# Dot-attention layers of a graph network: units in pairs for the weighted sum, and ScalarE's exponentials taken two units ahead

## The reference

```python
# layer 0, one head
Q, K, V = h @ W_q, h @ W_k, h @ W_v
scores = where(adj == 0, -1e9, Q @ K.T / 8)
x = x + softmax(scores) @ V
# layer 1, four heads
v, q, k = h @ Wv[i] + bv[i], h @ Wq[i] + bq[i], h @ Wk[i] + bk[i]
scores = leaky_relu(q @ k.T / 8, 0.2) + mask
x = x + leaky_relu(mean over heads of softmax(scores) @ v, 0.2)
# layer 2: additive attention; layer 3: a GAT layer with a residual and a layer norm
```

## Time and profile before

| what | value |
|---|---|
| median of 3 runs | 3531.48 us (3525.62 to 3535.83) |
| the profiled execution's own time | 3536.67 us |
| its span, first to last instruction | 3534.6 us |
| mean granted TensorE clock | 0.962 |
| TensorE matmul busy | 3064.6 us, 30972 instructions |
| VectorE busy | 3083.5 us |
| ScalarE busy | 2894.8 us |
| GpSimd busy | 1068.3 us |

### The profile page before, as it was taken

One profiled execution on the slowest core, in us unless ns is written; L12 is line 12 of the kernel. 1 busy time (PEld: TensorE's weight loads), 2 busy tenths in 40 slices (PEclk: granted clock), 3 DMA queues, 4 the chain that ended last, 5 costly groups with the idle time before them and its releaser, 6 DMA issues. The chain is left out here.

```text
span 3534.6 us, 78838 instructions
## 1 busy us (share of the span) xinstructions
PE 3064.6 (87%) x30972; PEld 1680.4 (48%) x30972; DVE 3083.5 (87%) x4791; ACT 2894.8 (82%) x3697; POOL 1068.3 (30%) x909
## 2 busy tenths in 40 slices
PE   7988999999999879898898898988988988987875
PEld 5765666666666633333333333333333333335664
DVE  7886887878888789999999999999999999985675
ACT  4546787778877769999999999998999999985665
POOL 4434666666666600000001000000001010006674
PEclk9998999999999989999999999999999999998797
DMA  7640000000000000000000000000000000002121
GB/s 246 222 139 16 20 21 22 21 18 24 21 21 19 14 10 10 10 10 10 10 10 10 10 10 10 10 10 10 10 10 10 8 9 10 13 4 68 58 60 33
DMA packets 68411, 111.58 MB, mean 32 GB/s; under 512 B 26452, under 2 KB 26582, under 8 KB 68054
## 3 DMA queue, kind: packets, MB, share of 16 engines
q1 hardware_dynamic: 68054, 106.69, 9.8%
HBM read 86.61 MB, written 18.87 MB: 30 GB/s over the span
## 5 line engine op out<-in xcount | busy, mean ns | idle before, releaser
L1107 ACT ACTIVATE l_scalar_ring<-l_w,l_r 128x1024 f32<-128x1024 f32 x1632 | 1713.1, 1142 | 37.5 <-DVE l_values L1153 27.7
L1221 DVE TENSOR_SCALAR l_vector_ring<-l_w_code,l_r_code 128x2048 f32<-128x2048 f32 x1232 | 1588.9, 1354 | 3.2 <-issue 0.2
L1044 PE MATMUL scores<-l_scalar_ring,l_signs 128*32 128x512 f32 x6528 | 793.5, 605 | 91.0 <-ACT l_scalar_ring L1107 90.7
L1054 PE MATMUL scores<-l_vector_ring,l_signs_code 128*32 128x512 f16 x9856 | 672.2, 394 | 138.3 <-DVE l_vector_ring L1221 137.6
L462 POOL TENSOR_TENSOR l_masked<-l_relu,mask 128x512 f32<-128x512 f32 x512 | 586.0, 1167 | 342.2 <-ACT l_relu L664 320.8
L250 ACT COPY probs_t<-turned 128x512 f32<-128x512 f32 x512 | 293.4, 586 | 467.1 <-PE turned L209 467.1
L1054 PEld LDWEIGHTS scores<-l_vector_ring,l_signs_code 128*32 128x32 bf16 x9856 | 242.7, 95 | 590.1 <-DVE l_vector_ring L1221 303.7
L277 ACT ACTIVATE l_probs<-l_logits,negmax 128x1024 f32<-128x1024 f32 x384 | 442.9, 1153 | 6.4 <-DVE negmax L268 6.4
L209 PE MATMUL turned<-ident,l_probs 128*128 128x128 f32 x3072 | 436.6, 287 | 12.1 <-issue 7.7
L1044 PEld LDWEIGHTS scores<-l_scalar_ring,l_signs 128*32 128x32 f32 x6528 | 200.0, 110 | 471.9 <-issue 264.8
L268 DVE CUSTOM_DVE_ANT_0 l_logits<-scores,l_masked,l_bound 128x1024 f32<-128x1024 f32 x256 | 328.1, 1282 | 63.2 <-POOL l_masked L462 42.8
(11 more groups left out here) (247 smaller groups left out, 3095.8 us busy)
## 6 DMA issues: line engine op xcount, KB each, us to landing
mask<-masks_kept SPq DMA_DIRECT2D x192, 256.0 KB, 2.6
l_adj<-adj SPq DMA_DIRECT2D x64, 512.0 KB, 5.9
masks_kept<-l_mask_ring SPq DMA_DIRECT2D x64, 256.0 KB, 4.8
x_res<-x SPq DMA_DIRECT2D x8, 256.0 KB, 5.1
out<-x_res SPq DMA_DIRECT2D x8, 256.0 KB, 2.9
l_h<-l_h SPq DMA_DIRECT2D x8, 128.0 KB, 2.9
l_kl<-l_dh SPq DMA_DIRECT2D x32, 2.0 KB, 1.8
l_kl<-l_dl SPq DMA_DIRECT2D x32, 2.0 KB, 1.8
```

Source lines behind the costliest of these rows:

```text
L1044: last = nc.tensor.matmul(s.scores[g * ROWS:(g + 1) * ROWS, buf, half, :], signs[:, window], scalar_ring[:, at % SCALAR_RING, g, halves[ha ...
L1054: last = nc.tensor.matmul(s.scores[g * ROWS:(g + 1) * ROWS, buf, half, :], signs_code[:, par, g % 2, window], parts(vector_ring[:, at % VE ...
L1107: last = nc.scalar.activation(scalar_ring[:, at % SCALAR_RING, g, :], w[:, par, :], ACT.Relu, bias=r[:, par, column:column + 1])
L1221: last = nc.vector.tensor_scalar(vector_ring[:, at % VECTOR_RING, g:g + 2, :], w_code[:, par, :, :], r_code[:, par, 0, column:column + 1], ...
```

## The change

It concerns the dot layers alone (`dot_layer` and `copy_half`), in four parts:

- **probs_t** of the dot layers is a buffer of their own with two slots, one for the even and one for the odd unit of a pair.
- **The weighted sum** is issued once in two units, at odd n. The even unit's sum stands in the lower 64 partitions of PSUM (column half 0), the odd one's in the upper; for each block of nodes the even unit's product is followed by the odd unit's. It waits for the half copies of both units.
- **One copy** of the sum (at odd n) and **one product** serve the pair. The product is issued after the turning of the next even n, and again at the graph's end. Its weights, `wv_pairs`, are 128 x 128 with the two heads' value weights on the diagonal (in layer 0 the same weights twice), so that 128 columns come out, 64 for each unit. VectorE finishes both units one after the other at even n, with a drain between them in layer 1.
- **The exponential** of ScalarE's iteration n is that of unit n+2; that of unit 1 is taken before the loop.

The order of VectorE's logits (n+2), ScalarE's relu (n+3), TensorE's scores (n+3), GpSimd's mask (n+3) and the fills is as before.

```diff
-def copy_half(eng, copy, s, sems, half, u):
+def copy_half(eng, copy, s, sems, half, u, to=None):
...
-    copy(s.probs_t[:, half * n:(half + 1) * n, :], s.turned[:, half * n:(half + 1) * n, :]
+    copy((s.probs_t if to is None else to)[:, half * n:(half + 1) * n, :], s.turned[:, half * n:(half + 1) * n, :]
...
+        wv_pairs = sb("wv_pairs", [P, PAIRED, P], F32)
+        probs_t = sb("probs_t", [P, 2, NB, P], F32)
...
-        unit_out = s.outT[:, P:P + D]
+        pair_out = s.outT[:, P:2 * P]
...
+            def turn_pair(q, p):
+
+                pe.wait_ge(sems["out_copied"], STARTS + q + 1)
+                wait(pe, sems["unit_done"], STARTS + 2 * q)
+                nc.tensor.matmul(pair_out, s.turned_out[:], wv_pairs[:, p % PAIRED, :], start=True, stop=True
+                                 ).then_inc(sems["out_turned"], 1)
+
+            def pair_times_values(par, q):
+
+                pe.wait_ge(sems["half0_copied"], STARTS + 2 * q + 2)
+                pe.wait_ge(sems["half1_copied"], STARTS + 2 * q + 2)
+                wait(pe, sems["out_copied"], STARTS + q)
+                wait(pe, sems["unit_done"], STARTS + 2 * q)
+                for j in range(NB):
+                    for odd in range(2):
+                        last = nc.tensor.matmul(s.outT[odd * D:(odd + 1) * D, 0:P], values[:, par, j, :], probs_t[:, odd, j, :],
+                                                start=(j == 0), stop=(j == NB - 1))
+                last.then_inc(sems["out_ready"], 1)
+
             def graph(b, par, project, last_graph):
                 for n in range(U):
                     u = b * U + n
                     turn_probs(pe, s, sems, probs[:, n % 2, :], u)
-                    if n > 0:
-                        turn_out(pe, s, sems, u - 1, 0, unit_out, weights=wv[:, (n - 1) % H, :])
+                    if n > 0 and n % 2 == 0:
+                        turn_pair(b * Q + n // 2 - 1, n // 2 - 1)
...
-                    wait(pe, sems["unit_done"], STARTS + u)
-                    if n == 0:
+                    if n == 1:
                         pe.wait_ge(sems["values_ready"], b + 1)
-                    probs_times_values(pe, s, sems, values[:, par, :, :], u)
-                turn_out(pe, s, sems, b * U + U - 1, 0, unit_out, weights=wv[:, H - 1, :])
+                    if n % 2:
+                        pair_times_values(par, b * Q + n // 2)
+                turn_pair(b * Q + Q - 1, Q - 1)
...
-                    copy_half(a, nc.scalar.copy, s, sems, 1, u)
-                    if not (last_graph and n + 1 == U):
-                        exponentials(a, s, sems, logits[:, (n + 1) % 2, :], probs[:, (n + 1) % 2, :],
-                                     (n + 1) % 4, u + 1)
+                    copy_half(a, nc.scalar.copy, s, sems, 1, u, probs_t[:, n % 2, :, :])
+                    if not (last_graph and n + 2 >= U):
+                        exponentials(a, s, sems, logits[:, n % 2, :], probs[:, n % 2, :], (n + 2) % 4, u + 2)
...
+            exponentials(a, s, sems, logits[:, 1, :], probs[:, 1, :], 1, 1)
...
-                    copy_half(v, nc.vector.tensor_copy, s, sems, 0, u)
-                    if n > 0:
+                    copy_half(v, nc.vector.tensor_copy, s, sems, 0, u, probs_t[:, n % 2, :, :])
+                    if n > 0 and n % 2 == 0:
+                        finish(b, n - 2, u - 2)
+                        if leaky:
+                            v.drain()
                         finish(b, n - 1, u - 1)
...
-                    copy_out(v, s, sems, u)
+                    if n % 2:
+                        copy_out(v, s, sems, b * Q + n // 2)
...
+                v.drain()
+                finish(b, U - 2, b * U + U - 2)
                 v.drain()
                 finish(b, U - 1, b * U + U - 1)
...
+            nc.vector.memset(wv_pairs[:], 0.0)
+            v.drain()
             v.wait_ge(sems["weights_in"], 16 * WEIGHT_LOADS)
+            for odd in range(2):
+                rows = slice(odd * D, (odd + 1) * D)
+                nc.vector.tensor_copy(wv_pairs[rows, :, rows], wv[rows, min(odd, H - 1):H:2, :])
```

More of the change, by code:

```diff
@@ L321, in dot_layer @@
     CONST = float(D)
+    PAIRED = max(1, H // 2)
+    Q = U // 2
     with ExitStack() as ctx:
@@ L759, in finish @@
                 slot = n % 4
-                v.wait_ge(sems["out_turned"], u + 1)
+                v.wait_ge(sems["out_turned"], b * Q + n // 2 + 1)
                 xb = s.block(b, i)
+                unit_out = pair_out[:, n % 2 * D:(n % 2 + 1) * D]
                 if not leaky:
```

## The result

The changed kernel takes 4171.69 us (median of 4 runs, 4158.55 to 4178.85), the kernel before 3533.65 beside it: a ratio of 1.179, with a 95% interval of 1.177 to 1.182. It is slower by 638 us. 4170 us was forecast, in a range of 4060 to 4290.

A forecast was written before the change was run, and what follows sets the result against it. The prediction took TensorE and VectorE in turn to bound layer 1 before, and a ring through three engines after. Terms 495 + 85 + 40 + 2 + 18 = 640 us gave 4170 us, 18% slower, range 4060 to 4290.

The forecast's parts named there:

- ring: Layer 1: logits u, exponential u, relu u+1, mask u+1, logits u+1, once per unit; 5.60 us a step, +495 us.
- steps after fills: Layer 1: evictions of the next graph's projection also wait behind logits; 6.17 us, or 7.04 before a fourth head; +85 us.
- layer 0: First dot layer, no relu or mask in chain: pair cycle 7.17 us, 34.0 us a graph against 28.63; +40 us.
- clock: TensorE's granted clock may fall to half in layer 1: +18 us taken, bounds nothing and 128 us.
- start-ups of layers 0 and 1 and their ends: Small operations at each layer's start, about +1 us in all, and a pair's sum ending layer 1, +1 us.
- layers 2 and 3: The two layers after the dot layers: untouched code, to take as long as now.
- Pairs cost nothing behind the ring: Layer 1, TensorE and VectorE: pairing's gains are covered by the ring, 2.9 us a pair spare; costed at nothing.
- rival C: Layer 1: logits do not wait on the mask, pairing saves 135 us, whole 3436 us; chance 0.04.
- half the mode switches: TensorE: halving tiling-mode switches saves up to 22 us where TensorE bounds, none by the ring.

The follow-up runs named there:

- experiment 2: Kernel before, units one by one, with only ScalarE's exponential moved to two units ahead in both dot layers: 4104.38 us.
- 3: Changed kernel with ScalarE's relu n+3 put ahead of its exponential n+2: 3810.3 us, ratio 1.077.
- experiment 9: Changed kernel with scores, relu, mask and logits also moved one unit further ahead, exponential still n+2: 3570.26 us, ratio 1.010.
- 4: Changed kernel with one more GpSimd add of 128x512 per unit of layer 1, written to a spare tile: 4373.86 us.
- experiment 6: Changed kernel with the first f16 product of each scores half issued twice, 0.43 us more TensorE work per unit: 4156.98 us.

## Why the prediction was right

Point by point, the profiled execution's 642.4 us (4177.0 less 3534.6):

| step | forecast | measured |
|---|---|---|
| ring, 253 steps | 495 (5.60 each) | 490 (5.58 each) |
| steps after fills | 85 | 86.1 (84 steps, 6.22 and 6.99 on average) |
| layer 0 | 40 | 42.1 (from the first to the last logits) |
| other steps of layer 1 over 5.58 (clock) | 18 | 11.4 |
| start-ups of layers 0 and 1 and their ends | 2 | 8.1 |
| layers 2 and 3 | 0 | 4.6 |

- **The ring** held within 0.03 us (5.61 read, 5.60 taken, 5.58 measured), since all four legs were in the trace once, in the start-up of layer 1, where nothing else covered them. Experiments 2 (it alone), 3 and 9 (opened in two ways) and 4 (stretched) show it as the cause.
- **Fills**: 6.17 and 7.04 were worked out, 6.23 and 7.01 are the medians. The step had three queues in it, of which the delay on VectorE is the one easily left out. One leg was not what the rows say: I took 0.73 from the eviction to VectorE's part, where the earlier trace rows has 0.93 with VectorE busy; in the fill step above it is 0.62.
- **Layer 0**: 34.0 us a graph worked out, 34.3 measured. My account gave the pair's sum and the exponential a cycle together; the two experiments with one of them alone give 29.3 and 32.5 us, thus 0.9 and 4.1 of the 5.9, and about 1 only together. So most of it is the exponential's.
- **Pairs cost nothing behind the ring**: true of the plain steps, 5.58 us with and without pairs. Of the 2.9 us a pair that I took as spare, experiment 6 shows 0.86 to be there (two times 0.43); the rest is not shown. Behind the ring the pairs did cost: against experiment 2, the steps after fills take 35 us more and layer 0 takes 13, which the forecast had in those two terms. And beside the ring I held the pairs for a gain that would show if it were gone (rival C took 135 us for it). **That part was wrong**: without the ring they cost 34 to 50 us. It counted the waits that pairing removes (the accumulator's 93.2 us) and set nothing against them; nor did the up to 22 us for half the mode switches show. Which new wait takes more than that back is open: TensorE's scores waiting for the logits and the sum for the odd half copy are the candidates of experiment 9.
- **Clock**: I took 18 us of at most 128, and even less is shown. The 169 steps of layer 1 without a fill add 11.4 over 5.58 each. The two longest of them (7.89 and 8.22 us, at the edges into the third and the fifth graph) make 5 of that and are no cost of the change: the kernel before has 8.45 and 8.20 us at the same two places. What is left, 6.4 us, is the most that the clock took from the plain steps. With the clock at 0.87, experiment 6 has 6.1 in place of the 11.4. The Trainium skill (TensorE: Matmul & The Clock Gate, Part 1) says that activity releases the throttle. Experiment 6 agrees: more work raised the clock of layer 1 from 0.82 to 0.87.
- **Start-ups and ends** were among the worst sized, 2 against 8.1: 1.1 up to the first logits of layer 0, 2.8 from its last logits to the start of layer 1, 2.7 from there to the first logits of layer 1, 1.6 at the end of layer 1. After the last logits of layer 0 a pair's sum took 3.44 us instead of 1.97. The start-up of layer 1 ran at a low clock in both kernels (0.61 from 302 to 350 us; 0.62 from 256 to 301 us before), so the clock doesn't tell why it grew.
- **Layers 2 and 3**: their code is unchanged, and the 4.6 us are within what it varies by: from the first to the last of the 128 logits operations that follow layer 1, the 13 profiled executions take from 2195 to 2214 us.

The total came out within 2 us of the measurement. That closeness is luck: the errors of the terms, +5, -1, -2, +7, -6 and -5, cancel, and each of them is a better measure of what was known. The mechanism, ring and fills, which make nine tenths of the sum, is not luck.

## What to carry to other kernels

Before taking an operation further ahead, look where in the iteration its input is made, and then at what stands behind it in its own queue: a wait at a queue's head hands its delay to every engine that is fed from that queue, and busy shares of 25% and 69% don't show it. A loop of waits through several engines is priced by one uncovered turn of it, which a layer's start-up often shows, divided by the units it spans; moving one of its operations by a unit changes that divisor. When a buffer's hand-over is done once for two units, look for the waits that are new, and not only for those that go.

## What the runs showed of the hardware

More work on TensorE, about 138 us of it, made the program no longer and raised the granted clock over layer 1 from 0.82 to 0.87; a longer ring lowered it to 0.76; and the same instructions without the ring ran at 0.99. I had not expected the clock to move so evenly with the idle share: it followed the waiting in all four and caused little of it.
